# Mixing stage: sixteen scatters of an image in pairs over eight tiles, and the landmark copies on ScalarE

## The chip, the cores and the metric

The kernel runs on one core of one Trainium2 chip. A core has five engines with instruction queues of their own: TensorE (PE; PEld is its weight load), VectorE (DVE), ScalarE (ACT), GpSimd (POOL) and SyncE (SP). They wait for each other through semaphores. The metric is the device time of one execution in microseconds; lower is better.

## The reference

The input is 16 images of 32x32 tokens with 128 channels. Three blocks follow one another: a windowed attention block with an MLP, a landmark (Nystrom) attention, and a layer of experts. The part that matters here is the end of the second block and the routing of the third:

```python
attn1 = softmax(einsum('bhnd,bhmd->bhnm', q, k_l))   # tokens x 64 landmarks, 8 heads
attn2_inv = _pinv(attn2)
out = attn1 @ (attn2_inv @ (attn3 @ v))
out = out + res                                       # depthwise convolution of v
t = t + out @ Wout + bout
# experts, on ln(t):
shared = sum of two dense experts on every token
top_v, top_i = top_k(softmax(t @ gate_w.T + gate_b), 2)   # two of eight experts
routed = sum over the two of top_v * expert(t)
t = t + shared + routed
```

## The kernel before

The program goes through its stages one after the other: set-up, attention in windows, MLP, landmarks, pseudo-inverse, mixing (`phase_mix`), experts. The change touches `phase_mix` alone.

The mixing stage takes an image (16 of them) as eight tiles of 128 tokens. Each engine runs the same loop over tiles `j` (image by image; `j.t` is 0 to 7) and calls `step(j)`, in which three images are worked on at once: `x = j + 8`, the next image, is prepared; `j` itself goes through attention; `y = j - 8`, the image before, is normalized and gated; `w = j - 16`, two images back, is sent to the experts. Order on an engine is the order of the code. `met(eng, s, q)` waits until signal `s` has been given for tile `q`; `known` does that for a whole image; neither waits where the tile is not real (before the first or after the last image). The first two iterations and the last are written out; in between stands a loop over two images at a time.

One tile goes through this chain. VectorE reduces a score bank to row maxima (L1803) and subtracts them (L1805). ScalarE takes the exponential (L1763). TensorE transposes it in four pieces (L1964, signal `eT_ok` only after ScalarE has copied it out, L1753). TensorE multiplies the copy by the landmark values `zd` (L2023). VectorE divides by the sum (L1813, L1815). TensorE transposes that (L1979), ScalarE copies it out (L1759), TensorE multiplies by the output weights (L2028, L2029), and VectorE adds the input rows (L1823, signal `t2_ok`). TensorE also computes the scores two tiles ahead (L1972), transposes the normalized rows (L1994) and computes the gate logits (L2049).

GpSimd has side work for each image: the power for the normalization (L1695, at `j.t` 0), two copies of 64x64 landmark values from `zA` into `zd` (L1706, `j.t` 1), an addition of the shared experts' bias to the rows that SyncE then stores (L1711, `j.t` 2), an addition of the output bias to the input rows of the next image (L1715, `j.t` 3), the split of the normalized rows into two float16 halves (L1723, L1725, `j.t` 3), a copy (L1729, `j.t` 5), and 16 scatters (L1737): indirect DMAs that GpSimd describes itself, each of 128 rows of 512 bytes to the places in `xs_dram` that the gate chose. They are issued at `j.t` 2 to 7 in lots of 2, 3, 3, 2, 3, 3 with no wait between them beyond those of the other work.

Of the kernel before, what the change touches and what calls it, by code (L numbers as in the profile page):

```python
# [24 lines left out]
ACT = mybir.ActivationFunctionType  # L25
# [8 lines left out]
NP = T // P  # L34
NH, HD = 16, 8
AH, AD = 8, 16
# [59 lines left out]
def build(nc, NB, A, out):  # L96

    _, _, _, KY, KX = window_constants()
    with ExitStack() as ctx:
# [23 lines left out]
        def apart(eng):  # L123


            eng.sem_inc(s_apart, 1)
# [1401 lines left out]
        def phase_mix(lnT, klA, zA, posA, wts):  # L1528
# [3 lines left out]
            with ExitStack() as c1:  # L1532
# [93 lines left out]
                def met(eng, s, q):  # L1626

                    if q.real():
                        eng.wait_ge(s.sem, (s.by * 16) * q.g + s.by * (q.k + 1))

                def known(eng, s, q, n=1):

                    if q.real():
                        eng.wait_ge(s.sem, (s.per * s.by * 2) * q.g + s.by * (s.per * q.odd + n))
# [17 lines left out]
                with nc.Block() as block:  # L1652
# [23 lines left out]
                    @block.gpsimd  # L1676
                    def _(gp):
                        n = 0
                        for k in range(2):
                            gp.memset(zd[k][:], 0.0).then_inc(zd_set, 1)  # L1680
                            n += 1
                        for k in range(2):
                            for half in range(2):
                                gp.wait_ge(zd_set, n)
                                gp.memset(zd[k][64 * half:64 * half + 64, :, half, AD:AD + 1], 1.0).then_inc(zd_set, 1)
                                n += 1
                        gp.wait_ge(zd_set, n)
                        gp.wait_ge(m_load, 16 * len(LOADS))
                        gp.wait_ge(b2s_ok, 1)

                        def step(j):
                            x, y, w = j + NP, j - NP, j - 2 * NP
                            if j.t == 0 and y.real():
                                known(gp, var_ok, y)
                                gp.tensor_tensor(rstd[:], rstd[:], nhalf[:, 0:NP], ALU.pow).then_inc(rstd_ok.sem, 1)  # L1695
                            if j.t == 1 and x.real():
                                met(gp, w_ps, j - 2)
                                old = w - NP
                                if old.real():
                                    gp.wait_ge(sent[old.odd].sem, sent[old.odd].at(old.g + 1, 0))  # L1700
                                    apart(gp)
                                for k in range(2):
                                    q = slice(64 * k, 64 * k + 64)
                                    if k:
                                        known(gp, zd_in, x, 1)
                                    gp.tensor_copy(zd[x.odd][q, :, k, 0:AD],  # L1706
                                                   zA[q, x.image(), :].rearrange("p (h d) -> p h d", h=4)).then_inc(zd_in.sem, 1)
                                known(gp, zd_in, x, 2)
                            if j.t == 2 and w.real():
                                known(gp, b_ok, w, 2)  # L1710
                                gp.tensor_tensor(rest[:], rest[:], b2s[:, 0, :].unsqueeze(1).to_broadcast([P, NP, C]), ALU.add)\  # L1711
                                    .then_inc(r_out.sem, 1)
                            if j.t == 3 and x.real():
                                known(gp, t_land, x)
                                gp.tensor_tensor(t_in[x.odd][:], t_in[x.odd][:], bout[:].unsqueeze(1).to_broadcast([P, NP, C]),  # L1715
                                                 ALU.add).then_inc(tb_ok.sem, 1)
                            if j.t == 3 and y.real():
                                known(gp, xn_ok, y, NP)
                                old = y - 2 * NP
                                if old.real():  # L1720
                                    gp.wait_ge(sent[y.odd].sem, sent[y.odd].at(old.g + 1, 0))
                                apart(gp)
                                gp.tensor_copy(xt16[y.odd][:, :, 0, :], xn[:]).then_inc(hi16_ok.sem, 1)  # L1723
                                known(gp, hi16_ok, y)
                                gp.tensor_tensor(xt16[y.odd][:, :, 1, :], xn[:], xt16[y.odd][:, :, 0, :], ALU.subtract)\  # L1725
                                    .then_inc(xtok_ok.sem, 1)
                            if j.t == 5 and y.real():
                                known(gp, hi_ok, y, 2)
                                gp.tensor_copy(x16[:, y.image(), 0:T], xh[:]).then_inc(keep_ok.sem, 1)  # L1729
                            if j.t >= 2 and w.real():  # L1730
                                if j.t == 2:
                                    known(gp, idx_ok, w)
                                    known(gp, xtok_ok, w)
                                    apart(gp)
                                for n in range(8 * (j.t - 2) // 3, 8 * (j.t - 1) // 3):
                                    t, k = n // 2, n % 2
                                    gp.indirect_dma_start(  # L1737
                                        out=xs, out_offset=bass.IndirectOffsetOnAxis(idxl[w.odd][:, k, t:t + 1], 0),
                                        in_=xt16[w.odd][:, t].rearrange("p h c -> p (h c)"), in_offset=None)\
                                        .then_inc(sent[w.odd].sem, 16)  # L1740

                        tiles(gp, step)
                        for k in range(2):
                            gp.wait_ge(sent[k].sem, sent[k].at(TURNS, 0))

                    @block.scalar
                    def _(ac):
                        def step(j):
                            x, y, w = j + NP, j - NP, j - 2 * NP
                            if j.real():  # L1750
# [18 lines left out]
                            if j.t == 1 and x.real():  # L1769
                                met(ac, w_ps, j - 2)  # L1770
                                ac.activation(lt[x.odd][:], lnT[:, x.image(), :], ACT.Copy).then_inc(lt_in.sem, 1)
                            if j.t == 2 and x.real():
                                for u in range(2):
                                    known(ac, qT_ps, x, u + 1)
                                    ac.activation(qT[x.odd][:, 512 * u:512 * u + 512], bank((1, 7)[u]), ACT.Copy)\
                                        .then_inc(qT_ok.sem, 1)
# [711 lines left out]
```

## Time and profile before

| what | value |
|---|---|
| runs of before | 4003.75, 4015.11, 4016.0 us; median 4015.11 us |
| profiled execution | span 4012.6 us from first to last instruction; no separate time is given for it |
| mean granted TensorE clock, whole span | 0.782 of full speed |
| PE / DVE / ACT / POOL busy | 3287.7 / 2411.7 / 1591.1 / 1145.0 us |
| mixing stage, first to last tile copy | 2172.3 to 2967.2 us |
| scatters of the mixing stage | 256, from 2244.8 to 3035.5 us |

The time is that of the slowest core, here the only one. The span is the profile's own, 2.5 us below the median of the runs. Times in rows are microseconds from the span's start; "[0.90 <-X]" behind a row of the timeline means that the engine had been idle for 0.90 us and that X ended the wait; "remote" stands where the semaphore moved but no instruction ended just then that could have moved it; "issue" where the profile shows nothing that was waited for.

### The profile page before, as it was taken

What the parts mean: (1) busy time and instruction counts of PE and PEld (TensorE: products, weight loads), DVE (VectorE), ACT (ScalarE), POOL (GpSimd) and SP (SyncE); (2) the same over time, 40 slices, a digit from 0 to 9 for tenths busy, and PEclk for the clock granted to TensorE, in tenths of its full rate; (3) what the DMA queues carried; (4) which work ended last, traced back from release to release, by engine and by line L of the source; (5) the groups of instructions that cost most, each with busy time, mean ns of one, the idle gap of its engine ahead of it and who ended that gap; (6) DMA issues with size and microseconds to landing.
All of it is one profiled execution on the core that took longest, in us unless ns stands there. A gap on an engine that the chain in (4) does not pass through costs nothing. (4 is left out here: it accounts for less than half of the span.)

```text
span 4012.6 us, 96955 instructions
## 1 busy us (share of the span) xinstructions
PE 3287.7 (82%) x35431; PEld 2392.7 (60%) x35431; DVE 2411.7 (60%) x6510; ACT 1591.1 (40%) x3175; POOL 1145.0 (29%) x1360
## 2 busy tenths in 40 slices
PE   2888888888887998999888888778864999877777
PEld 2555555655555765777777666556653666544444
DVE  2555555555554557888677766666664777555555
ACT  1444444444443433333102332223323777555554
POOL 0222222222222331111001455455452000244453
PEclk6655656565566998999899876776767999989888
DMA  2000000000001220000000111111113444222222
GB/s 83 15 16 17 16 17 16 17 16 17 16 14 39 72 66 26 21 21 16 3 4 21 34 42 42 36 37 40 40 35 86 97 96 97 75 64 64 64 64 56
DMA packets 298397, 162.23 MB, mean 40 GB/s; under 512 B 98300, under 2 KB 289160, under 8 KB 297736
## 3 DMA queue, kind: packets, MB, share of 16 engines
q1 hardware_dynamic: 281608, 123.16, 11.3%
q0 software_dynamic: 16384, 33.59, 2.8%
q8 instruction: 264, 4.33, 0.5%
q14 instruction: 141, 1.16, 0.1%
HBM read 66.74 MB, written 71.30 MB: 34 GB/s over the span
## 5 line engine op out<-in xcount | busy, mean ns | idle before, releaser
L2301 DVE TENSOR_TENSOR e_glo<-e_g,e_ghi 128x512 f16<-128x512 f32 x540 | 373.4, 692 | 270.3 <-ACT e_ghi L2208 195.9
L2203 ACT ACTIVATE e_g<-psum,b 128x512 f32<-128x512 f32 x540 | 369.7, 688 | 385.5 <-PE psum L2357 242.5
L2374 PE MATMUL psum<-w2hi,e_ghi 128*128 (+1 forms) x2160 | 415.5, 225 | 104.6 <-issue 54.5
L2187 POOL DMA_INDIRECT e_got<-ys_dram,e_idx x256 | 262.3, 1025 | 692.0 <-DMA ys_dram<-e_yo 422.6
L2378 PE MATMUL psum<-w2hi,e_glo 128*128 (+1 forms) x2160 | 410.9, 225 | 15.7 <-issue 15.0
L2376 PE MATMUL psum<-w2lo,e_ghi 128*128 (+1 forms) x2160 | 411.0, 225 | 6.0 <-issue 5.7
L2374 PEld LDWEIGHTS psum<-w2hi,e_ghi 128*128 128x128 f16 x2160 | 217.4, 101 | 243.9 <-issue 133.2
L592 DVE TENSOR_TENSOR pT<-pT,rpbx 128x512 f32<-128x512 f32 x128 | 89.9, 703 | 356.8 <-ACT pT L544 356.8
L1737 POOL DMA_INDIRECT xs_dram<-m_xt,m_idxl x256 | 257.0, 1004 | 116.2 <-issue 72.5
L479 POOL TENSOR_TENSOR rstd<-mv,eps 128x1 f32<-128x1 f32 x128 | 24.2, 189 | 825.5 <-DVE mv L637 825.5
L2376 PEld LDWEIGHTS psum<-w2lo,e_ghi 128*128 128x128 f16 x2160 | 217.8, 101 | 48.8 <-issue 14.8
L586 DVE TENSOR_REDUCE mx<-psum 128x16 f16<-128x1024 f32 x128 | 156.1, 1219 | 126.0 <-PE psum L663 125.9
L2208 ACT ACTIVATE e_ghi<-psum,b 128x512 f16<-128x512 f32 x334 | 228.0, 682 | 0.0
L2378 PEld LDWEIGHTS psum<-w2hi,e_glo 128*128 128x128 f16 x2160 | 218.7, 101 | 12.6 <-issue 12.5
L696 PE MATMUL psum<-vd,pT 128*64 128x18 f32 x4096 | 223.7, 262 | 0.0
L696 PEld LDWEIGHTS psum<-vd,pT 128*64 128x64 f32 x4096 | 209.6, 207 | 13.1
L2023 PEld LDWEIGHTS psum<-m_zd,m_p1T 128*128 128x128 f32 x1024 | 156.8, 234 | 95.0 <-issue 66.1
L2023 PE MATMUL psum<-m_zd,m_p1T 128*128 128x34 f32 x1024 | 164.0, 312 | 47.6 <-issue 33.5
L1972 PE MATMUL psum<-m_klm,m_qT 128*128 128x512 f32 x256 | 192.8, 848 | 0.0
L544 ACT ACTIVATE pT<-psum 128x512 f32<-128x512 f32 x256 | 139.9, 604 | 119.2 <-PE psum L680 119.1
L1753 ACT ACTIVATE m_p1T<-psum 128x512 f32<-128x512 f32 x128 | 76.6, 598 | 241.1 <-PE psum L1964 132.9
L492 POOL TENSOR_TENSOR pT<-pT,rpbx 128x512 f32<-128x512 f32 x128 | 162.0, 1266 | 22.2 <-ACT pT L544 22.2
(332 smaller groups left out, 8040.9 us busy)
## 6 DMA issues: line engine op xcount, KB each, us to landing
ys_dram<-e_yo SPq DMA_DIRECT2D x71, 256.0 KB
f_xm<-x_dram SPq DMA_DIRECT2D x32, 256.0 KB
mid_dram<-f_xm SPq DMA_DIRECT2D x32, 256.0 KB
l_t<-mid_dram SPq DMA_DIRECT2D x16, 512.0 KB
m_t<-mid_dram SPq DMA_DIRECT2D x16, 512.0 KB
res_dram<-m_rest SPq DMA_DIRECT2D x16, 512.0 KB
e_acc<-res_dram SPq DMA_DIRECT2D x32, 256.0 KB
out_dram<-e_acc SPq DMA_DIRECT2D x32, 256.0 KB
```

Of the source, the lines that this page charges most:

```text
L492: gp.tensor_tensor(p, p, e, ALU.mult).then_inc(pe_ok.sem, 1)
L696: i = pe.matmul(bank(7)[half(w), 2 * (HD + 1) * h:2 * (HD + 1) * (h + 1)], pT[:, q.odd, j, w, N * g:N * g + N], vd[:, q.u, 2 * q.odd + w, ...
L1737: gp.indirect_dma_start(out=xs, out_offset=bass.IndirectOffsetOnAxis(idxl[w.odd][:, k, t:t + 1], 0), in_=xt16[w.odd][:, t].rearrange("p h ...
L1972: pe.matmul(bank(2 + q.r), qT[q.odd][:, q.t * P:(q.t + 1) * P], klm[q.odd][:].rearrange("p h l -> p (h l)"), start=True, stop=True)\
L2023: i = pe.matmul(bank(6)[:, n * h:n * h + n], p1T[:, j.r, h, :], zd[j.odd][:, h].rearrange("p a d -> p (a d)"), start=True, stop=True)
L2187: gp.indirect_dma_start(out=got[:, q % 2, k, t, :], out_offset=None, in_=ys, in_offset=bass.IndirectOffsetOnAxis(idx[:, q // 2, i:i + 1], 0))\
L2203: ac.activation(g32[:, c % 4, :], bank(c % 4), ACT.Gelu, bias=bias, scale=1.0 / WSCALE)\
L2208: ac.activation(ghi[:, c % 4, :], bank(c % 4), ACT.Gelu, bias=bias, scale=1.0 / WSCALE)\
L2301: ve.tensor_tensor(glo[:, c % 4, :], g32[:, c % 4, :], ghi[:, c % 4, :], ALU.subtract)\
L2374: pe.matmul(o, ghi[:, c % 4, g], w2hi[:, e, f, :], start=first and t == 0, stop=False, skip_group_check=True)
L2376: pe.matmul(o, ghi[:, c % 4, g], w2lo[:, e, f, :], start=False, stop=False, skip_group_check=True)
L2378: i = pe.matmul(o, glo[:, c % 4, g], w2hi[:, e, f, :], start=False, stop=True, skip_group_check=True)
```

## The change

The two landmark copies go from GpSimd to ScalarE, behind its copy of `lnT` at `j.t` 1. ScalarE waits once, at its start, for the six memsets of `zd`. The 16 scatters of image `w` are issued two at a tile: twelve at `j.t` 2 to 7 and the last four at `j.t` 0 and 1 of the next image. The first of a tile waits for `eT_ok` of that tile, the second for `t2_ok` of the tile before it. The first scatter of an image also waits until all scatters of the image before have landed; that wait stood ahead of the landmark copies until now. Two steps are added behind the loop for the last four scatters.

```diff
-                            if j.t == 1 and x.real():
-                                met(gp, w_ps, j - 2)
-                                old = w - NP
-                                if old.real():
-                                    gp.wait_ge(sent[old.odd].sem, sent[old.odd].at(old.g + 1, 0))
-                                    apart(gp)
-                                for k in range(2):
-                                    q = slice(64 * k, 64 * k + 64)
-                                    if k:
-                                        known(gp, zd_in, x, 1)
-                                    gp.tensor_copy(zd[x.odd][q, :, k, 0:AD],
-                                                   zA[q, x.image(), :].rearrange("p (h d) -> p h d", h=4)).then_inc(zd_in.sem, 1)
-                                known(gp, zd_in, x, 2)
...
-                            if j.t >= 2 and w.real():
-                                if j.t == 2:
-                                    known(gp, idx_ok, w)
-                                    known(gp, xtok_ok, w)
-                                    apart(gp)
-                                for n in range(8 * (j.t - 2) // 3, 8 * (j.t - 1) // 3):
-                                    t, k = n // 2, n % 2
-                                    gp.indirect_dma_start(
...
+                            if j.t == 2 and w.real():
+                                old = w - NP
+                                if old.real():
+                                    gp.wait_ge(sent[old.odd].sem, sent[old.odd].at(old.g + 1, 0))
+                                known(gp, idx_ok, w)
+                                known(gp, xtok_ok, w)
+                                apart(gp)
+                            v, at = (w, j.t - 2) if j.t >= 2 else (w - NP, j.t + 6)
+                            if v.real():
+                                met(gp, eT_ok, j)
+                                apart(gp)
+                                scatter(v, 2 * at)
+                                met(gp, t2_ok, j - 1)
+                                apart(gp)
+                                scatter(v, 2 * at + 1)
 
                         tiles(gp, step)
                         for k in range(2):
+                            step(Tile(TURNS + 1, k))
+                        for k in range(2):
                             gp.wait_ge(sent[k].sem, sent[k].at(TURNS, 0))
...
+                        ac.wait_ge(zd_set, 6)
...
                                 ac.activation(lt[x.odd][:], lnT[:, x.image(), :], ACT.Copy).then_inc(lt_in.sem, 1)
+                                for k in range(2):
+                                    q = slice(64 * k, 64 * k + 64)
+                                    ac.activation(zd[x.odd][q, :, k, 0:AD],
+                                                  zA[q, x.image(), :].rearrange("p (h d) -> p h d", h=4), ACT.Copy)\
+                                        .then_inc(zd_in.sem, 1)
```

This is GpSimd's queue for one image of the mixing stage before the change, in the written-out iteration ahead of the loop, from `j.t` 0 to `j.t` 7. Numbers of buffers are left out; a semaphore in brackets bears the name that it had in an earlier stage (w_ve_ok is here `xtok_ok`, w_mv_ok `idx_ok`).

```order
L1695 TENSOR_TENSOR m_rstd<-m_rstd,nhalf 128x8 [waits w_stored2]
L1706 COPY m_zd<-zA 64x4x16 [waits w_newton,w_xb_ok]
L1706 COPY m_zd<-zA 64x4x16 [waits w_mT_ok]
L1711 TENSOR_TENSOR m_rest<-m_rest,m_b2s 128x1024 [waits w_onT_ps,w_mT_ok]
L1737 DMA xs_dram<-m_xt,m_idxl 135680x256 [waits w_mv_ok,w_ve_ok]
L1737 DMA xs_dram<-m_xt,m_idxl 135680x256
L1715 TENSOR_TENSOR m_t<-m_t,m_bout 128x1024 [waits s_po]
L1723 CAST m_xt<-m_xn 128x8x128 [waits w_v_ps,w_xb_ok]
L1725 TENSOR_TENSOR m_xt<-m_xn,m_xt 128x8x128 [waits w_h_ok]
L1737 DMA xs_dram<-m_xt,m_idxl 135680x256 x6
L1729 COPY lnT<-m_xh 128x1024 [waits w_rs_ok]
L1737 DMA xs_dram<-m_xt,m_idxl 135680x256 x8
```

And this is the same place of the changed kernel, from `j.t` 0 to the first scatter of `j.t` 3 (w_ss_ok is `eT_ok`; lines are numbered anew, L1720 is the scatter, L1698 the bias of the shared experts, L1702 that of the output, L1710 and L1712 the split).

```order
L1695 TENSOR_TENSOR m_rstd<-m_rstd,nhalf 128x8 [waits w_stored2]
L1720 DMA xs_dram<-m_xt,m_idxl 135680x256 [waits w_ss_ok]
L1720 DMA xs_dram<-m_xt,m_idxl 135680x256 [waits m_t2_ok]
L1720 DMA xs_dram<-m_xt,m_idxl 135680x256 [waits w_ss_ok]
L1720 DMA xs_dram<-m_xt,m_idxl 135680x256 [waits m_t2_ok]
L1698 TENSOR_TENSOR m_rest<-m_rest,m_b2s 128x1024 [waits w_onT_ps]
L1720 DMA xs_dram<-m_xt,m_idxl 135680x256 [waits w_ve_ok,w_xb_ok,w_mv_ok,w_ss_ok]
L1720 DMA xs_dram<-m_xt,m_idxl 135680x256 [waits m_t2_ok]
L1702 TENSOR_TENSOR m_t<-m_t,m_bout 128x1024 [waits s_po]
L1710 CAST m_xt<-m_xn 128x8x128 [waits w_v_ps,w_xb_ok]
L1712 TENSOR_TENSOR m_xt<-m_xn,m_xt 128x8x128 [waits w_h_ok]
L1720 DMA xs_dram<-m_xt,m_idxl 135680x256 [waits w_ss_ok]
```

The runs of six and eight scatters are gone: four stand ahead of the bias of the shared experts, two between the two bias additions, and behind the split come the second of `j.t` 3, two of `j.t` 4, the copy, and six of `j.t` 5 to 7, every one behind a wait of its own.

ScalarE's queue around `j.t` 1 before the change:

```order
L1767 ACTIVATE m_cwT<-psum 8x512
L1753 ACTIVATE m_p1T<-psum 128x512 [waits w_qn_ok,w_sq_ok]
L1759 ACTIVATE m_onT<-psum 128x128 [waits w_newton,w_pr_ok]
L1763 ACTIVATE m_e<-m_e 128x512 [waits w_qk_ps]
L1771 ACTIVATE m_lt<-lnT 128x1024 [waits w_newton]
L1753 ACTIVATE m_p1T<-psum 128x512 [waits w_qn_ok,w_sq_ok]
```

And of the changed kernel (L1774 is the copy of `lnT`, L1756 the copy of the transposed exponentials):

```order
L1770 ACTIVATE m_cwT<-psum 8x512
L1756 ACTIVATE m_p1T<-psum 128x512 [waits w_qn_ok,w_sq_ok]
L1762 ACTIVATE m_onT<-psum 128x128 [waits w_newton,w_pr_ok]
L1766 ACTIVATE m_e<-m_e 128x512 [waits w_qk_ps]
L1774 ACTIVATE m_lt<-lnT 128x1024 [waits w_newton]
L1777 ACTIVATE m_zd<-zA 64x4x16 x2
L1756 ACTIVATE m_p1T<-psum 128x512 [waits w_qn_ok,w_sq_ok]
```

Two instructions have come in between the copy of `lnT` and the copy of the next tile's transposed exponentials.

## Rows read from the trace of the kernel before

**Rows 1.** Windows, mixing stage and tail: length, PE, PEld, DVE, ACT, POOL busy, clock.
```profile
2172.30:2967.20 794.90, 657.30 (x3289) 479.71 (x3288) 515.87 (x1621) 255.25 (x529) 387.03 (x341) 0.75 0.12 38
2967.20:3036.50 69.30, 22.29 (x107) 18.11 (x107) 23.80 (x88) 5.57 (x12) 43.28 (x39) 0.50 0.14 46
```

**Rows 2.** Windows, last five tiles: image 1; image 4; sum of images 4 to 13.
```profile
2207.50:2231.90 24.40, 20.96 (x120) 16.39 (x119) 17.69 (x59) 9.12 (x21) 4.21 (x3) 0.83 0.00 1
...
2347.00:2380.70 33.70, 25.02 (x120) 18.34 (x119) 19.45 (x64) 9.12 (x22) 18.15 (x17) 0.75 0.08 28
sum 332.70, PE 250.30 PEld 183.97 DVE 195.21 ACT 91.53 POOL 184.67; mean PE 25.03 PEld 18.40 DVE 19.52 ACT 9.15 POOL 18.47
```

**Rows 3.** The same of images 2, 3 and 14 (sum), and four tiles of images 1 and 15.
```profile
sum 91.20, PE 71.63 PEld 53.31 DVE 59.15 ACT 27.60 POOL 57.58; mean PE 23.88 PEld 17.77 DVE 19.72 ACT 9.20 POOL 19.19
...
2207.50:2226.20 18.70, 17.50 (x101) 13.65 (x100) 12.16 (x35) 7.62 (x18) 4.21 (x3) 0.82 0.01 1
2942.50:2967.20 24.70, 17.05 (x99) 13.15 (x98) 15.26 (x52) 7.44 (x18) 18.17 (x17) 0.80 0.11 38
```

**Rows 4.** Timeline inside a run of scatters, image 9: start, length, engine, line.
```profile
2627.92 0.96 POOL L1737 DMA_INDIRECT xs_dram<-m_xt,m_idxl  x1 [0.30 <-issue]
2628.10 0.64 PE L1964 MATMUL psum<-ident,m_e 128*128 128x128 f32 x4
...
2629.18 0.95 POOL L1737 DMA_INDIRECT xs_dram<-m_xt,m_idxl  x1 [0.30 <-issue]
2629.43 0.27 PE L1979 MATMUL psum<-ident,m_on 128*128 128x128 f32 x1
...
2631.27 0.60 ACT L1753 ACTIVATE m_p1T<-psum 128x512 f32<-128x512 f32 x1 [5.68 <-remote]
...
2631.92 1.08 PE L2023 MATMUL psum<-m_zd,m_p1T 128*128 128x34 f32 x8 [2.21 <-issue]
...
2634.22 0.21 DVE L1813 RECIPROCAL m_r<-psum 128x8 f32<-128x8 f32 x1 [5.68 <-PE psum L2023]
```

**Rows 5.** Waits from 2232 to 2968 us: total, times, longest.
```profile
ACT m_p1T L1753 <- remote: 108.1, 26, 6.4
...
DVE m_r L1813 <- remote: 46.0, 10, 4.8
```

**Rows 6.** Timeline around two scatters that stand alone, image 8.
```profile
2560.32 1.06 POOL L1737 DMA_INDIRECT xs_dram<-m_xt,m_idxl  x1 [3.62 <-DVE m_idxl L1904]
...
2561.42 1.06 PE L2023 MATMUL psum<-m_zd,m_p1T 128*128 128x34 f32 x8
...
2561.68 0.96 POOL L1737 DMA_INDIRECT xs_dram<-m_xt,m_idxl  x1 [0.30 <-issue]
...
2562.51 0.21 DVE L1813 RECIPROCAL m_r<-psum 128x8 f32<-128x8 f32 x1 [1.05 <-PE psum L1979]
```

**Rows 7.** Single lines over the span: ns shortest/median/longest, first and last start.
```profile
L1737 POOL DMA_INDIRECT xs_dram<-m_xt,m_idxl x256: 954/958/1933, 2244.8 to 3035.5; - x128
...
L1715 POOL TENSOR_TENSOR m_t<-m_t,m_bout x16: 2342/2361/2374, 2166.9 to 2891.4; 128x1024 f32<-128x1024 f32 x16
...
L1723 POOL CAST m_xt<-m_xn x16: 1036/1036/1043, 2208.7 to 2990.5; 128x1024 f16<-128x1024 f32 x16
...
L1725 POOL TENSOR_TENSOR m_xt<-m_xn,m_xt x16: 2112/2132/2137, 2209.8 to 2991.6; 128x1024 f16<-128x1024 f32 x16
...
L1939 DVE TENSOR_SCALAR m_xn<-m_t,m_mv,m_rstd x128: 328/335/3132, 2206.4 to 2987.3; 128x128 f32<-128x128 f32 x128
```

**Rows 8.** Windows of the first three tiles of images 4 and 8.
```profile
2327.80:2347.00 19.20, 16.68 (x95) 12.35 (x94) 15.05 (x45) 7.23 (x14) 8.84 (x7) 0.82 0.21 63
2540.80:2565.20 24.40, 21.23 (x95) 15.35 (x95) 14.55 (x45) 7.22 (x14) 8.83 (x7) 0.64 0.17 49
```

**Rows 9.** Timeline of ScalarE at the second tile of image 9.
```profile
2609.87 1.05 ACT L1771 ACTIVATE m_lt<-lnT 128x1024 f32 x1
2611.38 0.60 ACT L1753 ACTIVATE m_p1T<-psum 128x512 f32<-128x512 f32 x1 [0.46 <-PE psum L1964]
```

More of the change, by code:

```diff
@@ L1729, in step, with scatter @@
                                 gp.tensor_copy(x16[:, y.image(), 0:T], xh[:]).then_inc(keep_ok.sem, 1)
-                            if j.t >= 2 and w.real():
-                                if j.t == 2:
-                                    known(gp, idx_ok, w)
-                                    known(gp, xtok_ok, w)
-                                    apart(gp)
-                                for n in range(8 * (j.t - 2) // 3, 8 * (j.t - 1) // 3):
-                                    t, k = n // 2, n % 2
-                                    gp.indirect_dma_start(
-                                        out=xs, out_offset=bass.IndirectOffsetOnAxis(idxl[w.odd][:, k, t:t + 1], 0),
-                                        in_=xt16[w.odd][:, t].rearrange("p h c -> p (h c)"), in_offset=None)\
-                                        .then_inc(sent[w.odd].sem, 16)
+                            def scatter(v, n):
+                                t, k = n // 2, n % 2
+                                gp.indirect_dma_start(
+                                    out=xs, out_offset=bass.IndirectOffsetOnAxis(idxl[v.odd][:, k, t:t + 1], 0),
+                                    in_=xt16[v.odd][:, t].rearrange("p h c -> p (h c)"), in_offset=None)\
+                                    .then_inc(sent[v.odd].sem, 16)
+                            if j.t == 2 and w.real():
[13 more added lines that the diff above has]
+                                scatter(v, 2 * at + 1)
                         tiles(gp, step)
+                        for k in range(2):
+                            step(Tile(TURNS + 1, k))
                         for k in range(2):
```

## The prediction

> **What bounds the kernel now.** I read the page first (the mixing stage is where the change is), then windows cut at the tile copies of ScalarE (L1753), then the timeline of single tiles, then the waits. The mixing stage runs 794.9 us over its tiles, and 69.3 us more go by until the last scatter [rows 1]. No engine fills it: PE is busy 657.3 of the 794.9, at a granted clock of 0.75, and GpSimd 387.0. So what counts is how long one tile's chain takes, and which wait ends last in it.
>
> The view that tells most is a comparison that the kernel makes by itself. Image 1 has the same work on PE, VectorE and ScalarE in its last five tiles (`j.t` 3 to 7) as later images, but no scatters yet, since no image is two behind it. Those five tiles take 24.4 us, with 120 PE, 59 DVE and 21 ACT instructions. In image 4 they take 33.7 us, with 120, 64 and 22, and 17 instead of 3 instructions on GpSimd; ten such images take 332.7 us, 33.3 each [rows 2]. The surplus is 332.7 - 244.0 = 88.7 us in these ten. In images 2, 3 and 14 it is 91.2 - 73.2 = 18.0, and in the four tiles that image 15 has to compare, 24.7 - 18.7 = 6.0 [rows 3]. Together 112.7 us: the most that these tiles can give back if nothing of GpSimd's got in the way.
>
> How a scatter on GpSimd delays a chain that does not need it is seen in the timeline. Inside a run of scatters PE ends its four transposes at 2628.10 + 0.64 = 2628.74, and ScalarE, idle, starts the copy that waits for nothing else at 2631.27: 2.53 us late. PE ends L2023 at 2633.00, and VectorE's reciprocal starts at 2634.22: 1.22 us late [rows 4]. The waits of the stage name these as "remote", for the signal comes when no PE instruction has just ended: 108.1 us in 26 waits of the tile copy and 46.0 in 10 of the reciprocal [rows 5]; these idle times begin before PE is done, so they are more than the lateness alone. Only signals of PE are late, and only while scatters follow one another. Two scatters that stand alone do nothing of the kind: with the second running from 2561.68 to 2562.64, PE ends L2023 at 2562.48 and VectorE goes on at 2562.51, 0.03 us later [rows 6]. So a pair is harmless, a long run is not, and in the runs read so the lateness starts at about the fourth scatter (2627.92 is the fourth of its run).
>
> The Trainium skill says otherwise: in "SBUF — State Buffer", section "Who interferes with whom", engines disturb each other only through the port pair that VectorE and GpSimd share, and TensorE and ScalarE never wait on anyone. By that rule the late signals would have another origin, and the sum below would be its last two terms alone; the 2.53 us beside the 0.03 us speak against it.
>
> **The change part by part.**
>
> *The runs are split into pairs.* Of the 88.7 us of surplus not all is lateness. VectorE has 64 instructions in the window instead of 59, 19.52 us instead of 17.69 [rows 2]: the cut falls earlier in its work, which is worth 1.8 us an image, 26 us over the 14 images. That leaves 112.7 - 26 = 87 us to be had, some 6.2 an image.
>
> *A run of four to six remains.* At `j.t` 2 and 3 GpSimd has, in its queue order, the bias of the shared experts, two scatters, the other bias, the split, two scatters. A scatter is 0.96 us and its successor starts 1.26 us after it [rows 4], 958 ns in the median [rows 7]; the additions are of one shape and take 2.36 each, the split 1.04 + 2.13 [rows 7]. That is 2 x 2.36 + 3.17 + 4 x 1.26 = 12.9 us. Two tiles at image 1's pace are 2 x 24.4 / 5 = 9.8 us [rows 2]. GpSimd so comes out of `j.t` 3 some 3 us behind the signals that it waits for, the waits are met already, and the scatters of tiles 3, 4 and 5 follow one another with the copy L1729 among them. Late signals there: below nothing, since pairs that fall out of step may never reach the fourth place; above, two signals of 2.53 us an image. I take 2.0 us an image, nearer to one such signal, because the tiles that follow are paced again: 28 us in 14 images, bounds 0 and 71. Gain so far 87 - 28 = 59.
>
> *PE's clock.* The first three tiles of an image take 19.2 us where the granted clock was 0.82 and 24.4 where it was 0.64, PE busy 16.68 and 21.23 us for the same 95 instructions [rows 8]; 24.4 also holds the turn of the loop, so I do not take the whole difference. In the last five tiles the clock is 0.83 in image 1 and 0.75 in image 4, where PE waits more [rows 2]. What a fuller PE gives back lies between nothing and half of the 4.55 us of PE time, 2.3 an image; I take 1.0, 14 us, bounds 0 and 32.
>
> *Scatters in tiles 0 and 1.* Four new ones there. The first two stand behind L1695, which waits for the normalization late in tile 0, so they run back to back into the first of tile 1: three in a row, which is the harmless length above. Cost nothing; if the fourth is close too, one signal of 1.22 us an image, 17 us.
>
> *Side work that is queued behind the waits.* L1711 (its result is stored by SyncE) and L1715 (needed an image later) come about a tile later; the split is needed an image later, and the copy L1729 by tile 3 of the next image. None is on the chain. Their place beside VectorE moves: L1939 takes 335 ns in the median and 3132 at the longest [rows 7], when it meets L1715. It may meet it less or meet a scatter instead; 3132 - 335 = 2.8 us an image either way, taken as nothing, 39 us at either bound.
>
> *The wait for the previous image's scatters* now stands at `j.t` 2 behind 2.36 us of L1711, with the last of them issued just ahead; the transfer is done by then. Nothing, and off the chain.
>
> *The landmark copies on ScalarE.* From 1.05 us for 1024 columns and 0.60 for 512 [rows 9] I estimate 0.15 us plus 0.06 for 64 columns, 0.2 each, 0.4 an image. They lie between the copy of `lnT` and the next tile copy, where ScalarE was idle for 0.46 us [rows 9]. Cover is just enough; taken 0.2 x 16 = 3 us, without the cover 6.4. GpSimd's 32 copies were off the chain: no gain.
>
> *The tail.* Behind the last tile GpSimd is what is waited for: 43.3 us busy in 69.3 [rows 1], 32 scatters. It now has the last four of image 13 as well, 4 x 1.26 = 5.0 us, partly while it would wait: 3 us.
>
> **Sum.** -59 - 14 + 3 + 3 = -67 us; from the span 4012.6 to 3946, and with the 2.5 us by which the median of the runs lies above that span, 3948 us.
>
> **The rivals.**
>
> *All lateness goes, and the clock comes back.* For it: pairs are clean, and a tile of image 1 is 4.9 us against 2.5 us for two scatters. Against: the side work of tiles 2 and 3. -87 - 32 - 17 + 6 gives 3885 us.
>
> *No gain: the delay belongs to scatters as such.* If each of the 16 costs what it costs today wherever it stands (8 us an image spread over 16, 0.5 us each), the late signals only move, and the last two terms remain: 4015 + 6 = 4021. The same time comes out if the signals are late for another reason than GpSimd. Against both: image 1 and [rows 6].
>
> *Slower: the signal makes the meeting certain.* The first scatter of a tile starts exactly when PE begins L2023, the second when PE is about to do L1979 and L1964, and this now in eight tiles instead of five. If the pair makes one signal late by 2.0 us in each tile, that is 16 us an image against the 8.0 of today (112.7 / 14): +8 x 14 = +112, some 4130 us. It decides from 1.0 us a tile on. For it: the lateness of 1.22 to 2.53 us is of that size; against it, the pair that VectorE passed with 0.03 us.
>
> **How the numbers follow.** A difference of 0.3%, 12 us, is about what a measurement of this kernel can tell from no change. The forecast has 0.65, all lateness gone 0.12, a smaller gain (GpSimd stays behind for most of the image: 71 of the 87 stay lost; -16 and +6 give 4005, with the clock's 14 us 3991) 0.09, no gain 0.07, slower 0.07. Faster by over 0.3% (under 4003) is the first three but a little of the third: 0.84; within it 0.08; slower 0.08. The range reaches from 3880, where all bounds of the gain meet, to 4002, inside the smaller gain; what lies outside it is the two last rivals and a little more.
>
> **What would show it.** Right: the last five tiles of images 4 to 13 take some 27 us each instead of 33.3; "remote" waits of the tile copy fall from 108 to under 50 us, and those that remain sit at the tiles 4 and 5, behind the split; the granted clock of the stage rises above 0.75; the ScalarE copies end before the tile's transposes. Wrong: late signals in every tile beside the first or second scatter of a lone pair; a GpSimd that runs behind its signals from tile 2 to tile 7; a longer L1939 beside a scatter; or a tail longer by over 10 us.

## The result, and the profile after

| comparison | kernel before | changed kernel | ratio, 95% interval |
|---|---|---|---|
| the first, 4 runs each | 4015.56 us (4003.75 to 4026.05) | 3977.94 us (3966.44 to 3984.9) | 0.9896 [0.9861, 0.9932] |
| on a second chip, 22 and 12 runs | 3970.25 us (3953.51 to 3993.41) | 3961.46 us (3949.61 to 3977.47) | 0.9985 [0.9961, 1.001] |

In the first comparison the change made the kernel 38 us faster, where 67 were forecast. On a second chip the kernel before is itself 45 us faster, and the change is worth nothing that can be measured. Both are looked at below; this section is about the first comparison, whose profiled execution took 3979.68 us with a span of 3977.9.

The windows of the changed kernel, cut as in [rows 1] and [rows 2]: the stage, the tail, the last five tiles of images 1, 8 and 9, and the sum of images 4 to 13. Columns: window, length, PE, PEld, DVE, ACT, POOL busy (instructions), granted clock, DMA share, GB/s.

```profile
2174.70:2912.10 737.40, 622.06 (x3289) 465.34 (x3287) 534.79 (x1608) 263.11 (x559) 382.70 (x306) 0.79 0.13 40
2912.10:2981.70 69.60, 20.53 (x108) 16.42 (x107) 26.47 (x100) 5.44 (x12) 49.78 (x45) 0.52 0.16 51
...
2210.90:2236.90 26.00, 22.51 (x120) 17.80 (x120) 17.80 (x60) 9.24 (x21) 4.21 (x3) 0.79 0.00 1
...
2550.80:2582.60 31.80, 24.56 (x120) 19.15 (x119) 22.03 (x64) 9.16 (x22) 18.88 (x16) 0.76 0.12 39
2601.50:2625.70 24.20, 20.41 (x120) 16.22 (x119) 18.88 (x60) 9.09 (x21) 17.32 (x15) 0.85 0.16 50
...
sum 285.30, PE 227.11 PEld 174.97 DVE 207.35 ACT 92.01 POOL 180.60; mean PE 22.71 PEld 17.50 DVE 20.73 ACT 9.20 POOL 18.06
```

The stage is 57.5 us shorter than in [rows 1], 47.4 of them in the last five tiles of images 4 to 13 (332.7 to 285.3). The reader should see two more things. VectorE is busy for 534.79 us instead of 515.87, although it does the same work. And the images are no longer alike: image 9 takes 24.2 us, as short as image 1 was in [rows 2], image 8 takes 31.8.

Of the late signals nearly nothing is left. These are waits of the stage, longest first; [rows 5] had 108.1 and 46.0 us of "remote", and the copy L1756 (L1753 before) and the reciprocal L1821 (L1813) now have none.

```profile
ACT m_p1T L1756 <- PE psum L1972: 155.7, 70, 6.4
ACT m_e L1766 <- DVE m_e L1813: 153.0, 61, 5.5
...
POOL xs_dram L1720 <- DVE m_t L1831: 113.0, 53, 4.1
...
DVE m_t L1831 <- remote: 1.6, 1, 1.6
```

What has grown is the second row: ScalarE waiting for VectorE (L1813, the subtraction ahead of the exponential). Before, it stood fourth:

```profile
ACT m_e L1763 <- DVE m_e L1805: 119.4, 48, 4.4
```

The timeline tells why: tiles 2 and 3 of image 8 first, then the same place in image 9 (start, length, engine, line).

```profile
2548.26 2.38 POOL L1698 TENSOR_TENSOR m_rest<-m_rest,m_b2s 128x1024 f32<-128x1024 f32 x1
2549.10 2.10 DVE L1940 TENSOR_TENSOR m_klm<-klA,headmask 128x512 f32<-128x512 f32 x1
2551.12 4.92 DVE L1947 TENSOR_SCALAR m_xn<-m_t,m_mv,m_rstd 128x128 f32<-128x128 f32 x8
2553.35 2.35 POOL L1702 TENSOR_TENSOR m_t<-m_t,m_bout 128x1024 f32<-128x1024 f32 x1
...
2599.86 0.87 DVE L1940 TENSOR_TENSOR m_klm<-klA,headmask 128x512 f32<-128x512 f32 x1
2600.66 2.13 DVE L1947 TENSOR_SCALAR m_xn<-m_t,m_mv,m_rstd 128x128 f32<-128x128 f32 x8
2603.34 0.97 POOL L1720 DMA_INDIRECT xs_dram<-m_xt,m_idxl  x1 [1.75 <-DVE m_xn L1947]
2604.32 2.37 POOL L1702 TENSOR_TENSOR m_t<-m_t,m_bout 128x1024 f32<-128x1024 f32 x1
```

In image 8 GpSimd's two additions (L1698 and L1702, L1711 and L1715 before) run beside VectorE's `klm` and `xn`, and these take 2.10 and 4.92 us. In image 9 a scatter happened to wait until `xn` was done, so the addition came behind it, and `xn` took 2.13. The eight pieces of `xn` stand ahead of the next tile's reduction on VectorE, so the 2.8 us go into the chain. Over the stage `xn` (the rows with 120 of its 128 pieces) takes 63.5 us instead of 37.0, while `klm`, which met the addition L1711 before as well, takes 20.9 instead of 27.0. First before, then after (count, busy time in us, mean ns):

```profile
L1939 DVE TENSOR_SCALAR m_xn<-m_t,m_mv,m_rstd 128x128 f32<-128x128 f32 x120 | 37.0, 377 | 0.0
```
```profile
L1947 DVE TENSOR_SCALAR m_xn<-m_t,m_mv,m_rstd 128x128 f32<-128x128 f32 x120 | 63.5, 611 | 0.0
```

The starts of the tile copies tell the two effects apart. In images 4 to 13 tiles 4 to 7 take 206.6 us together instead of 268.7, and tile 3, in which `xn` runs, 78.6 instead of 63.7.

ScalarE's landmark copies, against [rows 9]:

```profile
2544.06 1.05 ACT L1774 ACTIVATE m_lt<-lnT 128x1024 f32 x1
2545.00 0.52 ACT L1777 ACTIVATE m_zd<-zA 64x64 f32 x2
2545.55 0.60 ACT L1756 ACTIVATE m_p1T<-psum 128x512 f32<-128x512 f32 x1
```

The pair takes 0.52 us and ends just as the tile copy starts.

Last, the stage behind the mixing stage, whose code is unchanged, first before, then after:

```profile
3036.50:4012.60 976.10, 807.52 (x8107) 538.38 (x8107) 593.33 (x1134) 558.59 (x875) 263.29 (x257) 0.92 0.31 77
```
```profile
2981.70:3977.90 996.20, 820.99 (x8107) 546.67 (x8107) 594.22 (x1134) 558.47 (x875) 259.33 (x257) 0.90 0.30 75
```

It took 20.1 us more. So 864.2 - 807.0 = 57 us were gained in the mixing stage with its tail, 2.4 were lost ahead of it (it starts at 2174.7 instead of 2172.3), 20 behind it: 35 in the span.

### The profile page after: what moved, and what is told of

Read it like the earlier page. It is cut to its first block and busy times, and to the rows that moved or that the text cites. A ratio compares the mean times of both kernels' runs of the same rounds, so it can differ in the third digit from the quotient of the medians.

```text
span 3977.9 us, 97259 instructions
## 1 busy us (share of the span) xinstructions
PE 3269.3 (82%) x35431; PEld 2389.4 (60%) x35431; DVE 2433.7 (61%) x6510; ACT 1598.7 (40%) x3207; POOL 1142.1 (29%) x1328
## 5 line engine op out<-in xcount | busy, mean ns | idle before, releaser
L1720 POOL DMA_INDIRECT xs_dram<-m_xt,m_idxl x256 | 265.3, 1036 | 209.0 <-DVE m_t L1831 116.4
L479 POOL TENSOR_TENSOR rstd<-mv,eps 128x1 f32<-128x1 f32 x128 | 24.2, 189 | 824.6 <-DVE mv L637 824.6
L2031 PEld LDWEIGHTS psum<-m_zd,m_p1T 128*128 128x128 f32 x1024 | 154.5, 231 | 55.5 <-ACT m_p1T L1756 43.6
L1980 PE MATMUL psum<-m_klm,m_qT 128*128 128x512 f32 x256 | 182.6, 806 | 0.0
L769 PE MATMUL psum<-wqkT,xT 128*128 128x256 f32 x256 | 156.1, 712 | 1.4 <-ACT xT L530 1.4
```

The costliest lines, as they stand in the source:

```text
L1720: gp.indirect_dma_start(out=xs, out_offset=bass.IndirectOffsetOnAxis(idxl[v.odd][:, k, t:t + 1], 0), in_=xt16[v.odd][:, t].rearrange("p h ...
L1980: pe.matmul(bank(2 + q.r), qT[q.odd][:, q.t * P:(q.t + 1) * P], klm[q.odd][:].rearrange("p h l -> p (h l)"), start=True, stop=True)\
L2031: i = pe.matmul(bank(6)[:, n * h:n * h + n], p1T[:, j.r, h, :], zd[j.odd][:, h].rearrange("p a d -> p (a d)"), start=True, stop=True)
```

## The experiments

Two theories stood against each other at first. **A**: the runs of scatters hold up PE's signals, splitting them ends that, and a part of the gain is lost to GpSimd's additions meeting VectorE. **B**: tile 3 is long for another reason (PE's clock). Rivals came up on the way. The first four runs are on a chip where the kernel before takes 4013 us, the level of the first comparison (called the first chip here), the others on one where it takes 3970 to 3974 (the second).

**One addition moved (e1).**

```diff
-                            if j.t == 3 and x.real():
+                            if j.t == 6 and x.real():
                                 known(gp, t_land, x)
                                 gp.tensor_tensor(t_in[x.odd][:], t_in[x.odd][:], bout[:]...
```

> The changed kernel with one GpSimd instruction moved: the addition of bout to t_in (2.35 us, needed an image later) stands at tile 6 of the image instead of tile 3. Theory A (what the change gave back is partly lost again because this addition and the other one now meet VectorE's xn pieces and klm at tiles 2 and 3, which then take 4.9 instead of 2.1 us): tile 3 of images 4 to 13 falls from 7.7-9.1 us to some 5.5, and the time by 25 to 40 us, to 3940-3955. Theory B (tile 3 is long because of PE's half clock after the turn into the next image, whatever GpSimd does): tile 3 keeps its 7.7 us or more and the time stays at 3978 within 8.

Measured: 3934.37 us (before 4013.27), ratio 0.981 [0.9765, 0.9856]; 43.6 us less than the changed kernel in its own comparison, or about 35 by the two ratios to the kernel before. The stage and the last five tiles of images 4 to 13:

```profile
2171.30:2875.60 704.30, 597.61 (x3289) 445.91 (x3287) 504.01 (x1611) 261.90 (x559) 379.17 (x307) 0.83 0.14 42
...
sum 256.90, PE 209.24 PEld 160.15 DVE 187.19 ACT 90.95 POOL 180.36; mean PE 20.92 PEld 16.01 DVE 18.72 ACT 9.10 POOL 18.04
```

VectorE is at 504.01 us instead of 534.79, the clock at 0.83 instead of 0.79, the last five tiles at 25.7 each, and tile 3 of images 4 to 13 takes 58.9 us together instead of 78.6. Theory A holds and B falls: one instruction, moved by three tiles and changed in nothing else, was worth about as much as the whole change. Of the 44 us the traces have 32 in the mixing stage with its tail (807.0 to 704.3 + 70.9 = 775.2) and 9 in the experts' stage, whose code is the same.

**Both additions moved (e2).** As above, and `j.t == 2` of L1698 becomes `j.t == 4`, with SyncE's store.

> As the run before, and the addition of b2s to rest (2.38 us) moved from tile 2 to tile 4 too, with SyncE's store of it. Theory A: klm at tile 2 no longer takes 2.1 instead of 0.87 us; together with the other move 30 to 55 us less than the changed kernel, 3925-3950. Theory B: no move counts, 3978 within 8.

Measured: 3931.11 us, ratio 0.9789 [0.9759, 0.9818], an interval that lies wholly below that of the change (0.9861 to 0.9932). What `klm` and `xn` take in the changed kernel and in this one (ns shortest/median/longest):

```profile
L1940 DVE TENSOR_TENSOR m_klm<-klA,headmask x16: 673/1169/2189, 2167.0 to 2846.1; 128x512 f32<-128x512 f32 x16
...
L1947 DVE TENSOR_SCALAR m_xn<-m_t,m_mv,m_rstd x128: 329/335/3174, 2209.9 to 2928.4; 128x128 f32<-128x128 f32 x128
```
```profile
L1940 DVE TENSOR_TENSOR m_klm<-klA,headmask x16: 673/674/685, 2166.8 to 2796.5; 128x512 f32<-128x512 f32 x16
...
L1947 DVE TENSOR_SCALAR m_xn<-m_t,m_mv,m_rstd x128: 329/342/548, 2209.3 to 2873.0; 128x128 f32<-128x128 f32 x128
...
sum 248.50, PE 195.37 PEld 152.22 DVE 195.75 ACT 90.69 POOL 212.73; mean PE 19.54 PEld 15.22 DVE 19.57 ACT 9.07 POOL 21.27
```

No meeting is left on these two, and the last five tiles take 24.85 us, 0.45 above image 1 in [rows 2]: the whole surplus is gone. Of the time only 3 us more than e1 came, within its spread; in the profiles the mixing stage with its tail is 17 us shorter than in e1 (682.7 + 75.9 = 758.6).

**Without the signals (e4).**

```diff
-                                met(gp, eT_ok, j)
-                                apart(gp)
                                 scatter(v, 2 * at)
-                                met(gp, t2_ok, j - 1)
-                                apart(gp)
                                 scatter(v, 2 * at + 1)
```

> The changed kernel without GpSimd's two waits per tile for the signals: the scatters stand two to a tile over eight tiles in the program, but nothing paces them but what they stand behind. Theory A (PE's signals are late from about the fourth scatter of a run on): GpSimd runs ahead, from tile 3 on some ten scatters follow one another, the signals of PE in tiles 4 and 5 are late by 1 to 2.5 us again, and the time is 4000-4030. Rival C (the spreading in the program, or the copies on ScalarE, made the gain, not the signals): 3978 within 10.

Measured: 3959.46 us, ratio 0.9855 [0.9826, 0.9884]. A miss for theory A as I had put it: without any pacing the kernel is not slower than with it, as rival C had it. (Its stage is as long as the changed kernel's, 735.6 us between the first and the last tile copy after 737.4; the rest of the 18 us lies in the experts' stage. Within the stage it differs: the last five tiles of images 4 to 13 take 259.7 us instead of 285.3, the first three 236.4 instead of 212.7; why these are longer no run shows. `xn` takes 37.4 us, as before the change, and `klm` 32.2 instead of 20.9: without the waits the addition hardly meets `xn`, and `klm` is met more.) The trace shows runs of 4, 2, 4 and 6 scatters an image (the last two with L1716 between them) instead of 2, 6 and 8, and this is all the "remote" there is:

```profile
ACT m_p1T L1752 <- remote: 6.7, 3, 2.7
DVE m_r L1817 <- remote: 4.2, 2, 2.1
```

10.9 us against 154 in [rows 5], although a run of six stands in each of the 14 images that scatter beside attention. So moving four scatters into the next image's tiles 0 and 1 was enough to end most of the lateness; the waits for `eT_ok` and `t2_ok` were not what did it.

**Four behind a signal (e6).** `if j.t % 2 == 0:` wait for `eT_ok`, then four scatters back to back.

> The changed kernel with the scatters four to every second tile (2, 4, 6 and the next image's 0), back to back behind one signal of that tile. Theory A: the fourth of a run is just where lateness begins, so each run makes one signal late by 0 to 2 us; 56 runs give 20 to 60 us more, 3998-4035. Rival C (any pacing that lets scatters keep up with the tiles will do; the length of a run is of no account): 3978 within 10.

Measured: 3974.6 us, ratio 0.9899 [0.9866, 0.9933]; "remote" is one wait of 3.4 us. A run of four makes no more signals late than a pair: the start "at about the fourth" that I read from the trace was too early. The time is that of the changed kernel, but not tile by tile: the last five tiles of images 4 to 13 take 18 us less (267.3), the first three 19 us more (231.8). What makes the first three longer is open, here as in e4.

**The kernel before with the addition moved (e3).** In before, the addition L1715 goes behind the scatters of tile 7, where it splits no run.

> The kernel before, with one GpSimd instruction moved: the addition of bout to t_in stands behind the scatters of tile 7 instead of ahead of the split in tile 3, so that it splits no run of scatters. It asks what the meeting of this addition with VectorE's xn cost before the change. Theory A (port meeting, which the pacing made longer): before the change it cost less than after, so the gain here is less than the 43 us that the same move gave the changed kernel: 3985-4010, with the late signals of PE unchanged at 12 to 14 us an image. Theory B (the move is worth the same anywhere, and has nothing to do with the change): 3970.

Measured: 3977.21 us beside 3974.33, ratio 0.9996 [0.9971, 1.0021]. The move that is worth 35 to 44 us in the changed kernel is worth nothing here (the times expected assumed the first chip's level). That does not mean that the addition met nothing before the change. Beside before's profile on this chip (`before_again` below) tile 3 of images 4 to 13 is 19 us shorter (48.6 after 67.6), but the first three tiles are 16 us longer (223.9 after 208.0), tiles 4 to 7 14 us longer (240.3 after 226.4), and there are 132 us of "remote" at the three lines listed at the end instead of 81. So the meeting was there already, and the change made it longer, as the `xn` rows show; that it cost no time before is not shown.

**The landmark copies alone (e5).** Before's scatters, copies on ScalarE.

> The kernel before with the landmark copies on ScalarE alone: scatters in runs of 2, 6 and 8 as before, no signals; GpSimd's wait for the previous image's scatters moves from tile 1 to the first scatter of tile 2. Theory A: no gain in the scatters' lateness, 0.5 us of ScalarE an image beside its idle time: 4013 within 10. Rival C (part of the gain is GpSimd's freed time and its removed wait in tile 1): 3990-4003.

Measured: 3968.97 us beside 3974.33, ratio 0.9976 [0.9951, 1.0001]. No difference that can be told from none; this part of the change is neutral.

**Eight behind a signal (e7).** Both additions moved, and the scatters sent eight at `j.t` 2 and eight at 6.

```diff
+                                if j.t % 4 == 2:
+                                    met(gp, eT_ok, j)
+                                    apart(gp)
+                                    for n in range(2 * at, 2 * at + 8):
+                                        scatter(v, n)
```

> The kernel with both additions moved (rest at tile 4, t_in at tile 6; 3931 us), with the scatters sent eight back to back at tile 2 and eight at tile 6, each eight behind one signal. Theory A (signals of PE are late from about the fourth scatter of a run until 1.45 us behind its last): a run of eight holds up one or two signals, 2 to 4 us, two runs an image: 4 to 8 us an image, 55 to 110 us more, 3985-4040. Rival C (the length of a run is of no account, the gain came from the place of the scatters): 3931 within 10.

Measured: 3989.64 us beside 3974.33, ratio 1.0024 [0.9988, 1.006]; 80 us above the next run on the same chip, which differs only in how its scatters are spread and paced. Its timeline at the end of a run of eight, then its waits over the stage:

```profile
2498.11 0.98 PE L2030 MATMUL psum<-m_zd,m_p1T 128*128 128x34 f32 x8
2498.43 0.96 POOL L1720 DMA_INDIRECT xs_dram<-m_xt,m_idxl  x1 [0.30 <-issue]
...
2499.70 0.96 POOL L1720 DMA_INDIRECT xs_dram<-m_xt,m_idxl  x1 [0.30 <-issue]
...
2500.96 0.96 POOL L1720 DMA_INDIRECT xs_dram<-m_xt,m_idxl  x1 [0.31 <-issue]
2502.22 0.96 POOL L1720 DMA_INDIRECT xs_dram<-m_xt,m_idxl  x1 [0.30 <-issue]
2503.96 0.21 DVE L1820 RECIPROCAL m_r<-psum 128x8 f32<-128x8 f32 x1 [4.62 <-remote]
```
```profile
DVE m_r L1820 <- remote: 38.8, 10, 5.4
ACT m_xf L1791 <- remote: 38.5, 12, 4.0
DVE m_t L1830 <- remote: 15.8, 10, 2.9
ACT m_p1T L1755 <- remote: 9.9, 5, 4.2
```

PE ends L2030 at 2498.11 + 0.98 = 2499.09; the reciprocal, on a VectorE that has been idle for 4.62 us, starts at 2503.96, 4.87 us later and 0.78 us behind the end of the last scatter (2503.18). The additions are out of the way here, so this is the length of the run by itself. It rules out the rival that it is of no account, and since nothing but GpSimd's scatters and their waits differs, also that the late signals come from something other than GpSimd. How a scatter holds up a signal of PE, no run shows.

**Both additions moved, without the signals (e8).**

> The kernel with both additions moved (3931 us), without GpSimd's two waits per tile for the signals: two scatters to a tile in the program, paced only by what stands between them. Theory A: the additions, the split and the copy of xh, each a 1 to 3 us pause, now break the scatters into runs of two to six, and late signals of PE cost 1 to 2 us an image, while GpSimd runs ahead of the tiles and meets VectorE elsewhere: 3930-3960. Rival D (it is the signals that keep the meetings away from VectorE's long operations, so without them the additions meet xn again): 3965 or more.

Measured: 3909.56 us beside 3974.33, ratio 0.9817 [0.9774, 0.9859], the same as e2 within the intervals. Rival D falls. In one image the addition met another VectorE instruction, which shows that it is not `xn` that is special (L1950 takes 1.2 us elsewhere):

```profile
2491.34 4.07 DVE L1950 TENSOR_TENSOR lnT<-m_xf,m_xh 128x1024 f32 x1
...
2491.97 2.35 POOL L1702 TENSOR_TENSOR m_t<-m_t,m_bout 128x1024 f32<-128x1024 f32 x1
```

**Both kernels once more, on one chip.** No edit.

> The kernel before, unchanged, run once more, for its stages: on one chip its median was 4013 to 4016 us, on another 3974. Theory E (what differs from chip to chip and from run to run lies outside the change: the experts' stage took 967 to 996 us in ten profiles with the same code): the mixing stage is again within 10 us of its 864, and the difference lies in the experts' stage. Rival F (the mixing stage before the change is itself not steady, since the meetings on VectorE and the late signals fall differently each time): it comes out 20 us or more from 864.

> The changed kernel, unchanged, beside the one above on the same chip. Theory A with E: its mixing stage is within 10 us of 807, and the ratio of the times is 0.985 to 0.993. Rival F: its mixing stage comes out 20 us or more from 807, and the ratio is nearer to 1.

Measured: 3964.12 and 3961.46 us, beside 3970.25 for before in the same rounds; the changed kernel has 0.9985 [0.9961, 1.001]. Theory E fails for the kernel before: the mixing stage with its tail takes 744.8 + 69.8 = 814.6 us instead of 864.2. For the changed kernel it holds: 744.4 + 70.4 = 814.8, against 807.0. First the stage, the sum of the last five tiles, the experts' stage and the stage's "remote" waits of before on this chip, then stage, sum and experts' stage of the changed kernel:

```profile
2172.20:2917.00 744.80, 632.90 (x3289) 464.52 (x3288) 518.86 (x1609) 256.06 (x529) 397.27 (x340) 0.79 0.13 40
...
sum 294.10, PE 240.27 PEld 179.19 DVE 199.62 ACT 92.04 POOL 199.95; mean PE 24.03 PEld 17.92 DVE 19.96 ACT 9.20 POOL 20.00
...
2986.80:3951.90 965.10, 809.36 (x8107) 541.77 (x8107) 593.73 (x1134) 559.51 (x875) 262.72 (x257) 0.92 0.30 77
...
ACT m_p1T L1753 <- remote: 71.6, 14, 6.1
```
```profile
2177.50:2921.90 744.40, 618.44 (x3289) 464.81 (x3287) 533.71 (x1608) 263.09 (x559) 381.76 (x306) 0.81 0.13 40
...
sum 294.60, PE 234.28 PEld 181.64 DVE 208.06 ACT 92.40 POOL 182.82; mean PE 23.43 PEld 18.16 DVE 20.81 ACT 9.24 POOL 18.28
...
2992.30:3958.60 966.30, 806.51 (x8107) 540.50 (x8107) 593.65 (x1134) 558.80 (x875) 258.80 (x257) 0.92 0.30 77
```

On this chip the kernel before has 71.6 us of "remote" at the tile copy instead of 108.1 and none at the reciprocal, and its last five tiles cost 29.4 us each instead of 33.3. The changed kernel has none of that lateness on either chip, and the same meetings on both (VectorE 533.71 and 534.79 us). By the starts of the tile copies of images 2 to 15 the change makes tile 3 longer by 17.9 us here and by 20.4 there, and tiles 4 to 7 shorter by 21.4 here and by 78.5 there. So the meetings cost the same on both, and what differs is what the late signals cost before.

**The addition at tile 7, with and without the signals (e10, e11).** `j.t == 6` becomes 7 in e2 and e8.

> The changed kernel with the addition of b2s to rest at tile 4 and that of bout to t_in at tile 7, scatters behind the signals. Theory A (the additions do not meet klm or xn there): mixing stage 750 to 770, some 45 us less than the changed kernel, about 0.978 of the kernel before.

> The run above without GpSimd's two waits per tile. Theory A: the signals are not what counts; two scatters at a tile, with the additions, the split and the copy between them, stay in runs of up to four, so it is within 10 us of the run above. Rival G (the signals are needed to keep late signals of PE away): 20 us or more above it, with the lateness of PE's signals at 3 us or more an image.

Measured in the same rounds: 3921.78 us, ratio 0.9883 [0.9851, 0.9915], and 3922.36 us, 0.9886 [0.9849, 0.9924]. The signals make no difference (rival G falls). Both beat both kernels on this chip. Against my expectation the mixing stage of e10 is 696.6 + 76.1 = 772.7 us, and VectorE is at 530.61:

```profile
2174.50:2871.10 696.60, 573.22 (x3289) 427.01 (x3287) 530.61 (x1608) 261.62 (x558) 379.93 (x306) 0.84 0.14 42
```

At tile 7 the addition meets the comparisons of the gate (L1860, L1861) instead; L1861 takes 428 ns in the mean after 216 in the changed kernel:

```profile
L1861 DVE TENSOR_TENSOR m_gt<-m_lg 128x64 f32<-128x64 f32 x119 | 50.9, 428 | 0.0
```

VectorE pays nearly the same there, but the stage is 814.8 - 772.7 = 42 us shorter than the changed kernel's. That these comparisons are less often what the chain waits for is my reading, not shown.

## Why the prediction was right, and where it was not

For the first comparison the forecast was right in sign and mechanism, 30 us too low in time (3948 against 3977.94, inside its range). By its own steps:

- **Late signals of PE are what a long run of scatters costs, and splitting the runs gives them back.** Shown: "remote" waits are gone in the changed kernel, run e7 brings them back by length alone, e6 (runs of four) and e4 (runs of up to six) bound it from below. The residual of 28 us at tiles 3 to 5 was too much; next to nothing is left of it.
- **"Each behind a signal".** The prediction took the pacing for the means. It is the spreading: without the waits the time is the same or lower (e4 beside the changed kernel, e11 beside e10 in the same rounds). Side work that stands between the scatters splits the runs as well.
- **Side work, "taken as nothing", 39 us at either bound.** This is the term that was mis-sized: tile 3 of images 2 to 15 takes 20.4 us more. Moving L1702 away gives more than that back (32 us in the stage with its tail, 35 to 44 in the time), for a part of the meeting was there before. The row that told of it was at hand ([rows 7]: L1939 335 ns in the median, 3132 at the longest, when it meets L1715); I had no reason for zero beyond not knowing the sign. There was one: pacing ties GpSimd to the tiles, so that its additions at `j.t` 2 and 3 come when VectorE does its work of `j.t` 2 and 3; without the waits (e4) `xn` takes 37.4 us instead of 63.5. The Trainium skill says of this in "SBUF — State Buffer", section "Who interferes with whom", that VectorE and GpSimd share a port pair under an exclusive lock. By that a meeting costs up to the addition's length, and the trace agrees but for 0.4 us: 4.92 - 2.13 = 2.8 us beside a 2.35 us addition.
- **PE's clock in the first three tiles, -14.** Not seen: those of images 4 to 13 take 212.7 us together, from the starts of their tile copies, after 214.5. The stage's clock did rise, from 0.75 to 0.79, and it did so in the last five tiles.
- **Tail +3, ScalarE's copies +3.** Tail 69.6 instead of 69.3; the copies fit where they were put, and cost some 0.55 us each only in the second tiles of images 0 and 1 (2.90 to 3.46 and 4.08 to 4.63 us between tile copies), where the cover is missing. Run e5: no measurable effect.
- **The stage behind.** The sum had no term for it, and it took 20 us more in this profile. Over all 14 profiles it took 975 to 996 us on the first chip and 965 to 976 on the second, with the same code. On the second chip kernels with and without the waits lie alike. On the first the four with them lie at 987 to 996 and the two without at 975 and 976, one profile each; whether that is chance or an effect of the change stays open.

- **The rivals.** The slower one needed late signals beside lone pairs, the one without gain needed them to move along with the scatters; in the changed kernel there are none of either kind. The one in which all lateness goes was right about the lateness, and left out the meetings. Its sum has a slip: the 17 us of scatters in tiles 0 and 1 stood as a possible cost and are taken off as a gain. Without them it gives 3902 us instead of 3885, and the range would begin above 3880; the result is near neither.

In the sum the mixing stage with its tail gave 57 us where 67 were forecast. By the starts of the tile copies of images 2 to 15, tiles 4 to 7 gave 78.5 us (59 were forecast for the lateness), tile 3 took 20.4 more (nothing was forecast), the first three tiles gave 2.2 (14 for the clock); images 0 and 1 took 2.6 more (3 for the copies) and the tail 0.3 (3). That the sum of the stage came out so near is luck: a gain of 20 us too small and a cost of 20 us left out cancelled each other.

On the second chip the outcome is the "no gain" case by time, though not by its mechanism. What failed there is the first step, the surplus of 87 us read from [rows 2, 3]: one profile's surplus is not a property of the kernel alone. Before's last five tiles have 294.1 - 244.0 = 50 us of surplus there, and 88.7 in [rows 2]. The scatters themselves do not differ (median 962 ns against 958), so why fewer of PE's signals are late there stays open. That the time of before goes with the chip is inferred from the runs: all 11 runs of before beside the first four experiments and in the first comparison lie at 4003.75 us or above, all 59 of the unchanged kernel on the second at 4003.52 or below. That the lateness does so is less sure, for it rests on one profile each, here of before's fastest execution (3953.66 us), and it varies on the second chip too: e5, with the same runs of scatters, has 114.6 us of "remote" at the three lines listed below, before 80.7.

## What to carry to other kernels

When a change paces or moves one queue, ask for each instruction behind it what it will now run beside; here a 2.35 us addition that moved by a few microseconds made one tile of each image longer, 20 us in all, and moving it by three tiles returned these and more. Spread indirect DMAs that GpSimd issues between its other work: runs of four made next to no signal of another engine late, two runs of eight an image cost 80 us, some 3 us a run, and no wait is needed to spread them. A surplus read from one profile can be half as large in another, on another chip: run the unchanged kernel there before believing in a gain of a per cent.

## What the runs showed of the hardware that was not expected

- Signals of PE given while GpSimd issues indirect DMAs back to back reach ScalarE and VectorE late: in the run of eight shown above by 4.87 us, released 0.78 us behind the last scatter; nearly never in runs of up to four (3.4 us over the stage in e6), and seldom with a run of six in each image (10.9 us in e4), though the 2.53 us of [rows 4] fell into a run of six.
- How much of it the same kernel meets differs from profile to profile: 180.6 us of "remote" at three lines in one on the first chip and 80.7 in one on the second over the same stage, with scatters of the same length. Here is the third line, `onT`, of both; how much of the difference is the chip's is not shown.

```profile
ACT m_onT L1759 <- remote: 26.5, 16, 3.7
```
```profile
ACT m_onT L1759 <- remote: 9.1, 12, 0.9
```

(108.1 + 46.0 + 26.5 and 71.6 + 0 + 9.1.)
